# Running key and value states: plain fp32 matmuls per head into the lower and upper 64 output partitions

## What is computed

```python
z = cumlogsumexp(s, axis=time)
g = exp(z[t-1] - z[t]);  p = exp(s - z)
# step_k
hk = hk * g_t[None, :] + k_t[:, None] * p_t[None, :]     # state, 64 x 64
ok = q_t @ hk
pv = softmax(ok)
# step_v
hv = hv * g_t[:, None] + p_t[:, None] * v_t[None, :]     # state, 64 x 128
ov = pv @ hv
```

## Time and profile before

| what | value |
|---|---|
| runs, median (lowest to highest) | 1407.0 us (1406.31 to 1410.47) |
| profiled execution: span from its first to its last instruction | 1402.9 us |
| mean granted TensorE clock, share of full | 0.998 |
| TensorE matmul busy | 1370.4 us, 98% |
| TensorE weight load busy | 1197.8 us, 85% |
| VectorE busy | 951.8 us, 68% |
| ScalarE busy | 567.3 us, 40% |
| GpSimd busy | 336.4 us, 24% |

### The profile page before, as it was taken

How to read it: one execution, slowest core, us unless ns; L and a number is a source line. 1 busy time by engine, 2 the same in 40 slices (tenths; PEclk the granted TensorE clock), 3 DMA queues, 4 the chain that set the end, 5 groups by cost and what they waited for, 6 DMA issues and landing times. The chain is left out here.

```text
span 1402.9 us, 21964 instructions
## 1 busy us (share of the span) xinstructions
PE 1370.4 (98%) x7904; PEld 1197.8 (85%) x7904; DVE 951.8 (68%) x1812; ACT 567.3 (40%) x1562; POOL 336.4 (24%) x302
## 2 busy tenths in 40 slices
PE   7999999999999999999999999999999999999998
PEld 6888888888888888888888888888888888878886
DVE  6666776676776677767766776776676767755644
ACT  5344433454344443444334443444344443512210
POOL 3222412233223312331124222331223221210000
PEclk9999999999999999999999999999999999999999
DMA  6000100001000100010001000010000200000000
GB/s 202 9 1 1 51 3 17 0 23 31 16 1 23 30 17 0 2 52 1 16 1 36 17 16 1 23 31 16 1 21 25 61 31 1 1 1 31 30 31 31
DMA packets 35304, 31.78 MB, mean 23 GB/s; under 512 B 7568, under 2 KB 28048, under 8 KB 35216
## 3 DMA queue, kind: packets, MB, share of 16 engines
q1 hardware_dynamic: 35216, 30.44, 7.3%
HBM read 26.24 MB, written 4.19 MB: 22 GB/s over the span
## 5 line engine op out<-in xcount | busy, mean ns | idle before, releaser
L914 PE MATMUL p<-wvg_hi,xt_hi 128*128 128x512 f32 x512 | 210.2, 411 | 0.0
L916 PE MATMUL p<-wvg_hi,xt_lo 128*128 128x512 f32 x512 | 201.2, 393 | 0.0
L915 PE MATMUL p<-wvg_lo,xt_hi 128*128 128x512 f32 x512 | 200.4, 391 | 0.0
L523 ACT ACTIVATE v_tok<-p 128x256 f32<-128x256 f32 x128 | 49.3, 385 | 309.0 <-PE p L916 309.0
L914 PE MATMUL p<-xt_hi,wsqk_hi 128*128 128x512 f32 x384 | 150.5, 392 | 1.4 <-DVE xt_lo L857 1.4
L915 PE MATMUL p<-xt_lo,wsqk_hi 128*128 128x512 f32 x384 | 150.2, 391 | 0.0
L916 PE MATMUL p<-xt_hi,wsqk_lo 128*128 128x512 f32 x384 | 149.4, 389 | 0.0
L454 POOL TENSOR_TENSOR v_lo<-v_tok,v_hi 128x256 fp32r<-128x256 f32 x96 | 84.3, 893 | 195.9 <-ACT v_hi L532 195.9
L434 POOL TENSOR_TENSOR lhs_lo<-k_t,lhs_hi 128x512 fp32r<-128x512 f32 x32 | 41.1, 1284 | 313.3 <-ACT lhs_hi L518 313.3
L916 PEld LDWEIGHTS p<-wvg_hi,xt_lo 128*128 128x128 f32 x512 | 96.3, 188 | 22.5
L915 PEld LDWEIGHTS p<-wvg_lo,xt_hi 128*128 128x128 f32 x512 | 97.0, 190 | 16.7
(11 more groups left out here) (215 smaller groups left out, 3431.1 us busy)
## 6 DMA issues: line engine op xcount, KB each, us to landing
acc<-in_L_attn_hidden_states SPq DMA_DIRECT2D x4, 1024.0 KB, 7.5
raw<-in_L_attn_Wv SPq DMA_DIRECT2D x32, 128.0 KB, 2.4
raw<-in_L_attn_Wg SPq DMA_DIRECT2D x32, 128.0 KB, 2.8
raw<-in_L_attn_Wo SPq DMA_DIRECT2D x16, 256.0 KB, 2.8
out<-acc SPq DMA_DIRECT2D x16, 256.0 KB, 2.3
raw<-in_L_attn_Ws SPq DMA_DIRECT2D x8, 256.0 KB, 2.6
raw<-in_L_attn_Wq SPq DMA_DIRECT2D x8, 256.0 KB, 2.8
raw<-in_L_attn_Wk SPq DMA_DIRECT2D x8, 256.0 KB, 4.6
```

The costliest lines, as they stand in the source:

```text
L523: nc.scalar.activation(v_tok[:, c, :], PB[bk][:, 0:VW], ACT.Copy).then_inc(v_done, 1)
L914: nc.tensor.matmul(out_, lh, rh, start=(k == 0), stop=False)
L915: nc.tensor.matmul(out_, lh, rl, start=False, stop=False)
L916: last = nc.tensor.matmul(out_, ll, rh, start=False, stop=(k == n - 1))
```

## The change

`running_keys` and `running_values` become two plain fp32 matmuls each, one for each head. Head 0 has 64 weight columns and writes output partitions 0 to 63; head 1 has 64 weight columns and writes partitions 64 to 127. Both heads write the same columns of XB: 64 columns for the keys, 128 for the values. VectorE reads those compact columns twice, through a broadcast over the two heads, and multiplies by the same mask. The four tensors of halves, the two instructions that fill those of e and the six that fill those of v in each cell, and their semaphores go away. `running_values` waits for `v_done` from ScalarE in place of `v_lo_done`.

```diff
-            v_hi = early.enter_context(nc.sbuf_tensor("v_hi", [P, CH - 1, VW], F32R))
...
 # cell_gpsimd
-            pool.wait_ge(e_tok_hi_done, cell.count(1, 1))
-            nc.gpsimd.tensor_tensor(e_tok_lo[:]..., e_tok[:, 0:CH - 1, 1:3, :],
-                                    e_tok_hi[:]..., ALU.subtract).then_inc(e_tok_lo_done, 1)
-            for c in range(CH - 1):
-                pool.wait_ge(v_hi_done, cell.count(CH - 1, c + 1))
-                nc.gpsimd.tensor_tensor(v_lo[:, c, :], v_tok[:, c, :], v_hi[:, c, :].bitcast(F32),
-                                        ALU.subtract).then_inc(v_lo_done, 1)
...
 # cell_scalar
-            act.wait_ge(ok_summed, cell.count(1, 1))
-            nc.scalar.activation(e_tok_hi[:]..., e_tok[:, 0:CH - 1, 1:3, :], ACT.Copy).then_inc(e_tok_hi_done, 1)
-            values_high(act, cell, 0)
-            values_high(act, cell, 1)
...
-            values_high(act, cell, 2)
...
 # cell_vector
-                kept(dve, cell, c, hk_summed, hk_kept, hk[:, c, :], XB[:, 0:P], own[:, :, 0:M])
+                kept(dve, cell, c, hk_summed, hk_kept, hk[:, c, :].rearrange("p (h m) -> p h m", h=2),
+                     XB[:, 0:M].rearrange("p (a m) -> p a m", a=1).broadcast_to([P, 2, M]), own[:, :, 0:M])
...
-                kept(dve, cell, c, hv_summed, hv_hi_done, hv_hi[:, c, :], XB[:, P:P + VW],
-                     own[:].rearrange("p h n -> p (h n)"))
+                kept(dve, cell, c, hv_summed, hv_hi_done, hv_hi[:, c, :].rearrange("p (h n) -> p h n", h=2),
+                     XB[:, P:P + DV].rearrange("p (a n) -> p a n", a=1).broadcast_to([P, 2, DV]), own[:])
...
 # cell_tensor, running_keys
-                nc.tensor.matmul(XB[:, 0:P], k_tok[:, c, :], e_tok[:, c, 1:3, :].rearrange("p h m -> p (h m)"),
-                                 start=(c == 0), stop=True, skip_group_check=True).then_inc(hk_summed, 1)
+                for h in range(2):
+                    mm = nc.tensor.matmul(XB[h * DK:(h + 1) * DK, 0:M], k_tok[:, c, h * DK:(h + 1) * DK],
+                                          e_tok[:, c, 1 + h, :], start=(c == 0), stop=True, skip_group_check=True)
+                mm.then_inc(hk_summed, 1)
...
 # cell_tensor, running_values
-                pe.wait_ge(v_lo_done, cell.count(CH - 1, c + 1))
+                pe.wait_ge(v_done, cell.count(CH, c + 1))
...
-                    pe.wait_ge(e_tok_lo_done, cell.count(1, 1))
...
-                parts = ((e_tok_hi, v_hi), (e_tok_hi, v_lo), (e_tok_lo, v_hi))
-                for i, (e_part, v_part) in enumerate(parts):
-                    mm = nc.tensor.matmul(XB[:, P:P + VW], e_part[:, c, :], v_part[:, c, :],
-                                          start=(c == 0 and i == 0), stop=True, skip_group_check=True)
+                for h in range(2):
+                    mm = nc.tensor.matmul(XB[h * M:(h + 1) * M, P:P + DV], e_tok[:, c, 1 + h, :],
+                                          v_tok[:, c, h * DV:(h + 1) * DV], start=(c == 0), stop=True,
+                                          skip_group_check=True)
                 mm.then_inc(hv_summed, 1)
```

More of the change, by code:

```diff
@@ L264, in attention @@
         th = sb("th", [P, 2, VW])
-        with ExitStack() as early:
-            v_hi = early.enter_context(nc.sbuf_tensor("v_hi", [P, CH - 1, VW], F32R))
-            v_lo = early.enter_context(nc.sbuf_tensor("v_lo", [P, CH - 1, VW], F32R))
-            e_tok_hi = early.enter_context(nc.sbuf_tensor("e_tok_hi", [P, CH - 1, P], F32R))
-            e_tok_lo = early.enter_context(nc.sbuf_tensor("e_tok_lo", [P, CH - 1, P], F32R))
         y = sb("y", [P, CH, 2, DV])
@@ L329, in attention @@
         e_hi_done, e_lo_done = sem("e_hi_done"), sem("e_lo_done")
-        e_tok_hi_done, e_tok_lo_done = sem("e_tok_hi_done"), sem("e_tok_lo_done")
-        v_hi_done, v_lo_done = sem("v_hi_done"), sem("v_lo_done")
         osq_done, ovar_done, orstd_done = sem("osq_done"), sem("ovar_done"), sem("orstd_done")
@@ L446, in cell_gpsimd @@
                                     ALU.subtract).then_inc(e_lo_done, 1)
-            pool.wait_ge(e_tok_hi_done, cell.count(1, 1))
-            nc.gpsimd.tensor_tensor(e_tok_lo[:].rearrange("p c (h m) -> p c h m", h=2), e_tok[:, 0:CH - 1, 1:3, :],
-                                    e_tok_hi[:].rearrange("p c (h m) -> p c h m", h=2).bitcast(F32),
-                                    ALU.subtract).then_inc(e_tok_lo_done, 1)
-            for c in range(CH - 1):
-                pool.wait_ge(v_hi_done, cell.count(CH - 1, c + 1))
-                nc.gpsimd.tensor_tensor(v_lo[:, c, :], v_tok[:, c, :], v_hi[:, c, :].bitcast(F32),
-                                        ALU.subtract).then_inc(v_lo_done, 1)
             if J is not None:
@@ L528, in values_scalar @@
                                  scale=0.5).then_inc(th_done, 1)
-        def values_high(act, cell, c):
-            act.wait_ge(v_done, cell.count(CH, c + 1))
-            nc.scalar.activation(v_hi[:, c, :], v_tok[:, c, :], ACT.Copy).then_inc(v_hi_done, 1)
         def y_high(act, cell, half):
@@ L564, in cell_scalar @@
                 y_high(act, cell, 1)
-            act.wait_ge(ok_summed, cell.count(1, 1))
-            nc.scalar.activation(e_tok_hi[:].rearrange("p c (h m) -> p c h m", h=2), e_tok[:, 0:CH - 1, 1:3, :],
-                                 ACT.Copy).then_inc(e_tok_hi_done, 1)
-            values_high(act, cell, 0)
-            values_high(act, cell, 1)
             act.wait_ge(ok_less_top, cell.count(1, 1))
@@ L799, in cell_vector @@
                     cols = slice(h * DV, (h + 1) * DV)
-                    low = nc.vector.scalar_tensor_tensor(out=hv_lo[:, c, cols], in0=XB[:, P + h * DV:P + (h + 1) * DV],
+                    low = nc.vector.scalar_tensor_tensor(out=hv_lo[:, c, cols], in0=XB[:, P:P + DV],
                                                          scalar=own[:, h, 0:1], in1=hv_hi[:, c, cols].bitcast(F32),
```

## The result

The kernel after takes 1443.86 us (median of 4 runs, 1442.96 to 1445.14); the kernel before took 1406.88 us beside it. The ratio is 1.0267, with a 95% interval of 1.0251 to 1.0283: slower by 37 us. The profiled execution after has a span of 1443.4 us, 40.5 us above the span of before; its own time was 1445.14 us. The forecast was slower, 1462.3 us; the direction was right, and the amount (+55 us) half as much again as measured (+37).

What follows compares the result with a forecast made beforehand. TensorE's queue was taken as the bound. Narrow passes -7.2, changes of array form +63.4 and the first cell -0.9 sum to +55.3 us on 1407.0, giving 1462.3 us; range 1383 to 1500.

Steps and rivals of the forecast that it cites:

- What bounds the kernel: TensorE's queue is the path, its matmul row 98% busy; work taken off GpSimd and ScalarE counts for nothing.
- The change of form: Entering and leaving 64-column matmuls at six calls a cell: 384 changes at 0.165 us of lost overlap, +63.4 us.
- rival C: Each change of form exposes both overlap and weight load, 0.27 us: 1503 us, or 1519 with passes in series; chance 0.22.
- the first thing to check: Distance from the last 512-column matmul to a call's first pass: about 0.39 us if overlap is lost, 0.226 if not.
- My argument against an open load: On TensorE, a start after a wait took 0.25 us to the next start against 0.22 in sequence, only 0.03 more.
- A sign I had named: TensorE's busy share falls below 98% by gaps at the key and value calls, with no engine named for them.
- The passes: Four narrow passes per key or value call cost three pass-times: -0.055 and -0.02 us, 96 calls each, -7.2 us.
- Rival A: At the six calls in each cell, form changes are free and heads run fully side by side: 1383 us; chance 0.20.
- break-even: With the full side-by-side gain, 0.062 us per change of form: below that the kernel gets faster, above it slower.
- First cell: TensorE's wait for v_lo goes, but it then waits for hv_kept from VectorE: -0.9 us, at most 1.7 back.
- The sum: -7.2 + 63.4 - 0.9 = +55.3 us for the whole kernel, giving 1462.3 us.
- the forecast's own range: 1437 to 1485 us, for 0.10 to 0.20 us per change of form, passes in parallel or not; chance 0.45.

Runs made afterwards that it cites:

- same-half kernel: Kernel after, with head 1 written to the same lower half of the output partitions as head 0, for keys and values: 1475.78 us, ratio 1.0498.
- one-group kernel: Kernel after, with key sums and value sums of chunks 0 and 1 in one narrow group per cell, chunk 2's value sum one wide matmul: 1404.17 us.
- extra-narrow kernel: Kernel before, plus one unused plain fp32 matmul of 64 weight columns by 64 columns ahead of each key sum: 1450.46 us, ratio 1.0297.

## Why the prediction was right, and where it was off

**What bounds the kernel.** Right. The work of GpSimd and ScalarE is not what moves this kernel: 157 us less on those two engines brought nothing that shows, and what the timelines show on a state call came out about 96-fold at the end (0.08 us gave 10.5, 0.32 gave 32).

**The change of form.** Right in size; its make-up was not as I had it. I took 0.165 us for each of 384 changes, from the overlap of a matmul with the next, 0.33 for a pair and 63.4 us in all. The narrow matmul by itself gave 0.35 us for a pair, and the calls of the kernel after give 0.47 - 0.11 = 0.36 and 0.57 - 0.21 = 0.35: about 67 us. The ceiling of 0.54 for a pair (rival C) was too high. But I had named as the first thing to check a distance of about 0.39 us to the first pass of a call, the whole drawn length of the matmul in front. It is 0.32: 0.09 us are lost before the first pass begins, where I took 0.165. And the weight load, which I left hidden and gave to rival C, does stand open, on the way in and on the way out. So the price is made of both, gaps and open loads, and together they are less than rival C had; how the 0.35 us divides between them is not shown. That their sum lies so near the 0.33 of a lost overlap is partly luck.

My argument against an open load was a misreading of the earlier trace rows. I compared 0.25 us behind the wait with 0.22, the next start after running_keys(2). But the first start behind a hole is early, and the call behind the wait is running_keys(1), with other work after it. Taken to the second matmul behind the call, it stands so, behind the wait and then in step (kernel before):

```profile
34.29 0.49 PE L993 MATMUL xb<-e_tok,k_tok 128*128 128x128 f32 x2 [0.63 <-DVE hk L728]
...
34.74 0.28 PE L915 MATMUL s<-bd_lo,lhs_hi 128*128 128x256 f32 x1
...
107.14 0.38 PE L993 MATMUL xb<-e_tok,k_tok 128*128 128x128 f32 x2
...
107.48 0.28 PE L915 MATMUL s<-bd_lo,lhs_hi 128*128 128x256 f32 x1
```

That is 0.45 against 0.34: a start on an empty engine costs 0.11 us there, not 0.03. A sign I had named did not come either: TensorE's busy share stayed at 98%.

The Trainium skill, "TensorEngine Tiling (Array Packing)", Key Properties, says that changing the tiling mode drains TensorE. These runs agree: about 0.35 us for each pair of changes.

**The passes.** This is the step that failed. I wrote that of four passes "only the two in the middle belong to different heads and can lie beside each other", so three pass-times, -0.055 for a key call and -0.02 for a value call, -7.2 us in all. The same-half kernel shows two pass-times: 0.11 against 0.22 for the keys and 0.21 against 0.36 for the values, 96 x (-0.11 - 0.15) = -25 us. That is the lower bound that I had given, -23.0, and my argument from program order against it was wrong. The term was mis-sized by 18 us. The form came out 4 us dearer than I took it, so by the spans the forecast was 15 us too high (55.3 against 40.5). By the medians it was 18 too high (1462.3 against 1443.9); the difference between the two comes from which executions were profiled. Rival A was right about the heads and wrong about the form; its break-even, 0.062 us per change, was passed almost threefold (0.35 / 2 = 0.175).

**First cell.** I took -0.9 us, between 0 and -1.7. From one group of e transposes to the next the first cell took 36.43 us before and 36.52 after, where an ordinary cell grew by 1.25: -1.2 us. The wait went from v_lo to hv_lo, as forecast, and the clock fell to half behind it again.

**The sum.** 67 - 25 - 1 = 41, against 37.0 between the medians and 40.5 between the spans. One stretch of the spans' difference is not the change's, and with it the sum would be 42.6; the 2 us too many are in part those of running_keys(2), whose call grew by 0.19 us and not by 0.24. The stretch: the profiled execution after has a second stay at the half clock, behind a jump of the loop. Windows of it: us, PE, PEld, DVE, ACT, POOL busy, granted clock, DMA:

```profile
686.00:688.00 2.00, 0.84 (x4) 0.85 (x5) 0.18 (x2) 0.72 (x6) 1.00 (x1) 0.81 0.64 192
688.00:690.00 2.00, 2.00 (x9) 1.80 (x8) 1.23 (x5) 1.19 (x2) 0.64 (x1) 0.50 0.32 79
690.00:692.00 2.00, 2.00 (x9) 1.56 (x9) 0.93 (x4) 0.00 (x0) 0.00 (x0) 0.84 0.00 0
```

That cell is 1.6 us longer than its neighbours; the medians of the runs, 37.0 us apart, are less touched by it.

**The range and the chances.** 1443.9 lies inside 1383 to 1500 and inside the forecast's own range, 1437 to 1485. That own range is not what its conditions give: a price of 0.10 with full parallelism is 1407 + 38.4 - 23.9 = 1421.5, and 0.20 with the passes in series is 1491.5. The measured time lies in both.

## What to carry to other kernels

Splitting a wide matmul into per-head narrow ones halves the streaming, because the halves of the array run side by side, but every entry and exit of the narrow form costs about 0.35 us here: it pays only where many narrow matmuls stand together. Before splitting, count the changes of form, not the columns; then gather the narrow matmuls into one place, even at the price of adding up on VectorE afterwards. Gathered, the same narrow matmuls gained 0.5% here where scattered they lost 2.7%. And when a stretch of the bounding engine is shortened, look at who has work to finish in that same stretch: the one-group kernel lost its gain to the engine that was only 70% busy.

## What was not expected of the hardware

- Four passes issued as head 0, head 0, head 1, head 1 take two pass-times. In the kernel after, the key group is 0.34 us long and its shortest pass is drawn 0.222, so the last of the four starts at most 0.12 us after the first. The records do not name the head, so which two run together cannot be read.
- The plain fp32 passes of these runs fit the larger of two times: about 0.11 us with 128 weight columns, or about 0.85 ns for each streamed column (0.107 to 0.109 us for 128 and 0.22 for 256). So 64 streamed columns with 128 weight columns still cost 0.23 us for two passes, while the narrow passes of 64 columns, at 0.053, were cheaper than any pass of before. Whether the weight columns or the form sets the 0.11 is not shown: they change together in every run.
- The form has to be read from the profile's shape column (128*64): the busy share of the matmul row stayed at 98% while 0.35 us were lost 192 times, since the drawn length of a matmul covers the hole. The signs in the trace are "issue" idle time on the weight-load row and the distance of 0.32 us where 0.227 is the step.
- The jump of the loop leaves TensorE idle for up to 2 us, and in some executions the clock granted behind it is half for a stretch that costs 1.6 us. It scatters the runs: the extra-narrow kernel ran in 1444.6 to 1455.2 us, with a mean granted clock of 0.999 in the fastest and 0.992 in the slowest, which has three cells longer than their neighbours by 1.6 us. Why the clock falls behind some jumps and not behind others stays open: the kernel after has two jumps with 2.00 us of idle TensorE, before 687.15 and before 844.94, and only the first is followed by a longer cell.
